# An attention and mixture-of-experts block on one core: the third batch's chain to token parts run between the second batch's expert units

## The chip, the cores and the metric

One core of a Trainium2 chip. The time is that of the whole program on the device in microseconds (us); less is better. Engines: TensorE (PE), VectorE (DVE), ScalarE (ACT), GpSimd (POOL) and SyncE (SP), which issues most of the DMAs. Each engine runs its own instructions in order and waits on semaphores for the others.

## The reference

For each of four batches of 512 tokens of width 128: causal attention with 16 heads of 8, then 16 experts of which two are mixed for each of 8 slices of 16 of a token.

```python
h = _layernorm(x) * (1 + ca) + sa
x = x + ga * _L0_attn_ref(h, Wq, bq, Wk, bk, Wv, bv, Wo, bo)     # rope, causal softmax, 16 heads
h = _layernorm(x) * (1 + cb) + sb
x = x + gb * _L0_ffn_ref(h, Wm, bm, expert_emb, W1, b1, W2, b2, Wo, bo)
# in _L0_ffn_ref:
t = (x @ Wm + bm).reshape(bs * L_ * H, HD)
w = softmax(t @ expert_emb); topw, topi = top_k(w, 2)
hmid = gelu(einsum('td,edi->tei', t, W1) + b1); eo = einsum('tei,eio->teo', hmid, W2) + b2
out = (take_along_axis(eo, topi) * topw).sum(axis=1).reshape(bs, L_, d) @ Wo + bo
```

## The kernel before

The order on each engine is written out by hand. After an opening, the kernel alternates two kinds of stage: the softmax of one batch and the expert units of the batch before it. `("loop", b)` for b = 0 and 1 is the softmax of batch b + 1 and then the expert units of batch b; `("late", 2)` is the softmax of batch 3 and then the expert units of batch 2; `("last", 3)` is the expert units of batch 3. Batches are counted from 0 in the code, so the second batch is batch 1, the third is batch 2 and the fourth is batch 3.

In a softmax stage TensorE makes scores (`big<-q_dense,k_block`) in 24 units, ScalarE takes the exponential of each into a ring of 8 buffers (L701), and TensorE weighs the values with them (`acc<-ring,vals`). Two groups of eight key blocks follow each other; `between[(g, blk)]` is a step put after the scores of block blk of group g. Between them runs what turns a batch's attention output into what its experts need, called the chain here:
- `turn_output`: TensorE transposes y (`misc<-ident,y`), VectorE copies the result to yT (L995);
- `project_out` (`misc<-wog,yT`) and `residual` (x1, L1002), `statistics` (L872 to L883), GpSimd's reciprocal root (L585), `normalise` (xn, L891 to L897);
- `turn_residual` (`misc<-ident,xn`), `modulate` (rot, L906), `tokens` (`misc<-rot,cb`; tf, L1010, cut into three bf16 parts by L910 to L913), the parts stacked by DMAs (`tstack<-tp`);
- `logits` (`misc<-cb,tf`), `route` on VectorE (L1028 to L1056, 16 instructions) with ScalarE's exponential ex (L730), `routed` (`misc<-ident,second`), wT (L1064), and 16 DMAs that spread the weights (`gm<-wT`).

In an expert stage 16 half-steps t run: TensorE makes two hidden units (`big<-tstack,w1s`), ScalarE their gelu into the ring, TensorE the outputs n = t - 2 (`acc<-ring,cb`), which VectorE (even n, L1079) or ScalarE and GpSimd (odd n, L741 and L623) multiply with the spread weights in gm. At t = 12 (`CB0_AT`) and at the end TensorE combines them (`misc<-gm,cb`), VectorE copies the result to combT (L1068), and after the last product (`misc<-wofg,combT`) VectorE adds the sum into lg (L1093) for the store. In the expert stages of batches 0 and 1 the maxima of batch b + 2 run as well, three units per half-step (`CHUNKS`): TensorE fills a bank (`misc<-k_dense,q_block`), VectorE reduces it (mx, L956). Units of all kinds share the two banks of `misc` in the order that `MISC` lists; `wait_bank_free` makes TensorE wait until the last but one use of the list is read. In the expert stage of batch 2 there are no maxima, and the chain of batch 3 (`"tail"`, `TAIL_AT`) runs there already.

The start of batch 3's softmax on VectorE (L1159 to L1171) is the yT copy, a memset of 32 rows of k_dense (L1161), the rest of the chain, the routing and the division of the attention sums. GpSimd there folds the gates: L604 and L606 (experts), L585 (the root), L592 to L595 and L612.

Of the kernel before, what the change touches and what calls it, by code (L numbers as in the profile page):

```python
# [32 lines left out]
NB, T, D = 4, 512, 128  # L33
# [6 lines left out]
NG = 2  # L40
GP = NP // NG
VW = P // GP
FH, FD, NE, FI = 8, 16, 16, 64
# [39 lines left out]
TURN_AT, ROUTE_AT = 16, 20  # L83
# [11 lines left out]
HALVES = 2 * len(STEPS)  # L95
# [15 lines left out]
TAIL_ROUTE_AT = 30  # L111
PREPARE = ["xT", "ue", "uo"]
# [23 lines left out]
at = 0  # L136
# [7 lines left out]
def opening():  # L144
# [9 lines left out]
    for k, part in enumerate(parts):  # L154
        wide = k in (1, 3)
        for use in part:
            n = len(uses)
            banks.append(n % 4 if wide else n % 2)
            if wide and banks[-1] > 1:
# [8 lines left out]
MISC = {"first": OPENING,  # L168
        "loop": ["yT", "ao"] + PREPARE + ["x1T", "tT", "lg", ("oT", 0), "wT", ("oT", 1), "v0", "v1"]
                + [use for t in range(2, HALVES + 2) for use in ["cb0"] * (t == CB0_AT) + CHUNKS[t]] + ["cb1", "fo"],  # L170
        "late": ["yT", "ao", "x1T", "tT", "lg", ("oT", 0), "wT", ("oT", 1)]
                + [("tail", use) for _, use in sorted((at, use) for use, at in TAIL_AT.items())]
                + ["cb1", ("tail", "wT"), "fo"],
        "last": ["cb0", "cb1", "fo"]}
MISC["late"] = [use if use != ("tail", "cb0") else "cb0" for use in MISC["late"]]
MISC_N = len(MISC["loop"])

MISC_START = {"first": 0, "loop": len(MISC["first"])}
MISC_START["late"] = MISC_START["loop"]
MISC_START["last"] = MISC_START["late"] + len(MISC["late"]) - MISC_N  # L180
assert MISC_N % 2 == 0

# [44 lines left out]
def build(nc, x, pack_a, pack_b, pack_c, w1_rows, shift_ones, out):  # L227
    with ExitStack() as ctx:
# [82 lines left out]
        yT_of = [yT[:, :]] * (NB - 1) + [freed[:, 0:T]]  # L311
        lg_of = [lg[:, :, :]] * (NB - 1) + [freed[:, T:2 * T].rearrange("p (n e) -> p n e", e=NE)]
# [28 lines left out]
        def use_of(here, name):  # L341
            if here[0] == "tail":
                return MISC_START["late"] + MISC["late"].index(("tail", name)) - MISC_N
            if here[0] == "second":
                return MISC["first"].index(("second", name))
            return MISC_START[here[0]] + MISC[here[0]].index(name)
# [8 lines left out]
        def wait_bank_free(eng, here, name):  # L355
# [6 lines left out]
            eng.wait_ge(s["misc_read"], here[1] * MISC_N + use_of(here, name) + 1)  # L362

        def wait_filled(eng, here, name):

            eng.wait_ge(s["misc_filled"], here[1] * MISC_N + use_of(here, name) + 1)

        def wait_read(eng, here, name):

            eng.wait_ge(s["misc_read"], here[1] * MISC_N + use_of(here, name) + 1 + CREDIT["misc_read"])  # L370
# [1243 lines left out]
```

## Time and profile before

| | |
|---|---|
| median of 3 runs | 431.77 us (429.78 to 432.44) |
| profiled execution | 431.06 us, span 429.2 us |
| mean granted TensorE clock | 0.939 |
| TensorE busy | 356.3 us (83%) |
| VectorE busy | 286.6 us (67%) |
| ScalarE busy | 257.9 us (60%) |
| GpSimd busy | 101.9 us (24%) |
| chain of waits | TensorE 54%, VectorE 15%, ScalarE 10% of the span |

How to read it: the busy shares are averages over stages with different bounds; what a step is worth is read from the timeline of its own stage. In a timeline each row is one instruction, or several alike merged (x with the count), with its start, its length, its engine, line and operands; in square brackets at the end stands how long the engine was idle before it and what ended that. A float32 matmul shows as two (x8 for four).

### The profile page before, as it was taken

To read this page: it belongs to the slowest core of one execution; us is meant where nothing else is said; L and a number is where in the kernel's file an instruction comes from. 1 tells how busy PE (TensorE), PEld (TensorE's weight loads), DVE (VectorE), ACT (ScalarE), POOL (GpSimd) and SP (SyncE) were. 2 spreads that over 40 slices of the span, in tenths; PEclk is the share of its full clock that TensorE was granted. 3 is DMA by queue.
4 is the path that set the end of the run, shared out by engine and by line. 5 is a ranking of instruction groups with operands and counts; after the bars stand their busy time and mean duration, and the time that the engine had idled before them with its cause. 6 is when DMAs were issued, how large, how long until landed. Compare 5 with 4: busy or idle time off the path is not lost.

```text
span 429.2 us, 7252 instructions
## 1 busy us (share of the span) xinstructions
PE 356.3 (83%) x2652; PEld 162.1 (38%) x2684; DVE 286.6 (67%) x593; ACT 257.9 (60%) x299; POOL 101.9 (24%) x149
## 2 busy tenths in 40 slices
PE   3745879778679889998889799998697899689994
PEld 3412434435345443433545344344354223132122
DVE  4847946888787958776676877764749247933332
ACT  9264043522247868875439858765457787858970
POOL 6080200105250204433232024431500042122000
PEclk9965868999899989999989999999989899989999
DMA  7253000003201715550105345530013256504550
GB/s 266 80 91 69 18 26 3 2 2 54 27 2 38 111 48 134 144 137 9 28 2 97 51 117 134 144 78 3 26 33 42 63 140 170 96 2 130 145 138 30
DMA packets 26991, 31.43 MB, mean 73 GB/s; under 512 B 6470, under 2 KB 17734, under 8 KB 26950
## 3 DMA queue, kind: packets, MB, share of 16 engines
q1 hardware_dynamic: 23740, 28.71, 28.7%
q0 software_dynamic: 3072, 2.13, 2.8%
q8 instruction: 21, 0.34, 0.4%
q10 hardware_dynamic: 144, 0.13, 0.1%
q14 instruction: 14, 0.11, 0.1%
HBM read 3.47 MB, written 1.05 MB: 11 GB/s over the span
## 4 chain that ended last, share of the span: by engine, by line
PE 54%; DVE 15%; ACT 10%; issue 7%; SPq 5%; DMA 5%; POOL 3%; ACTq 0%; POOLq 0%; DVEq 0%
PE acc L1193 18%; PE misc L1193 17%; PE big L1193 17%; ACT ring L701 7%; DVE mx L956 4%; PE misc L1215 2%; DVE xn L897 2%; DMA q_dense<-qk 2%; SPq L401 2%; SPq L448 2%; SPq L469 2%; DMA q_dense<-nm 1%; ACT qk_turned L709 1%; DMA gm<-wT 1%; DVE stats L872 1%
## 5 line engine op out<-in xcount | busy, mean ns | idle before, releaser
L701 ACT ACTIVATE ring<-big 128x1024 f32<-128x1024 f32 (+1 forms) x224 | 198.0, 931 | 129.5 <-PE big L1193 128.4
L956 DVE TENSOR_REDUCE mx<-misc 128x1 f32<-128x512 f32 (+7 forms) x151 | 86.1, 591 | 34.3 <-PE misc L1193 32.7
L1193 PE MATMUL acc<-ring,cb 128*32 128x512 f32 x512 | 68.8, 613 | 5.4 <-ACT ring L701 4.4
L1193 PE MATMUL big<-tstack,w1s 128*128 128x512 bf16 x177 | 54.7, 396 | 9.1 <-ACT ring L701 6.9
L1193 PE MATMUL big<-q_dense,k_block 128*128 128x448 bf16 (+7 forms) x249 | 55.0, 324 | 4.2 <-DMA gm<-qk_turned 2.0
L1079 DVE SCALAR_TENSOR_TENSOR gm<-acc,cb,gm 128x512 f32<-128x512 f32 x40 | 29.9, 747 | 27.6 <-DMA gm<-wT 20.0
L1193 PE MATMUL misc<-k_dense,q_block 128*128 128x320 bf16 (+7 forms) x168 | 42.9, 318 | 5.1 <-DVE mx L956 4.7
L1193 PE MATMUL acc<-ring,vals 128*32 128x64 f32 (+7 forms) x512 | 43.2, 436 | 0.4
L1193 PEld LDWEIGHTS big<-q_dense,k_block 128*128 128x128 bf16 x256 | 30.9, 149 | 31.0 <-ACT ring L701 14.0
L1193 PEld LDWEIGHTS misc<-k_dense,q_block 128*128 128x128 bf16 x171 | 20.7, 149 | 52.1 <-DVE mx L956 37.1
L1193 PE MATMUL big<-earlier_query,identb 128*128 128x64 bf16 (+2 forms) x176 | 37.5, 213 | 2.6 <-DMA q_dense<-nm 1.8
L623 POOL TENSOR_TENSOR gm<-osb,gm 128x512 f32<-128x512 f32 x12 | 15.6, 1298 | 93.7 <-ACT osb L741 60.7
L1193 PE MATMUL misc<-later_key,identb 128*128 128x64 bf16 (+2 forms) x151 | 32.3, 214 | 5.7 <-DMA q_block<-qk_turned 5.5
L401 POOL DMA_DIRECT2D k_block<-qk_turned x48 | 28.3, 593 | 0.5 <-issue 0.4
L1193 PEld LDWEIGHTS big<-tstack,w1s 128*128 128x128 bf16 x192 | 13.3, 98 | 33.3 <-ACT ring L701 21.8
L623 POOL TENSOR_TENSOR gm<-yT,gm 128x512 f32<-128x512 f32 x12 | 15.3, 1274 | 40.5 <-ACT yT L741 37.9
L709 ACT COPY qk_turned<-qk 128x512 bf16<-128x512 bf16 x12 | 12.2, 1088 | 14.6 <-DVE qk L913 14.6
L1193 PEld LDWEIGHTS big<-earlier_query,identb 128*128 128x128 bf16 x176 | 20.5, 116 | 1.0 <-issue 0.9
L1193 PEld LDWEIGHTS acc<-ring,cb 128*32 128x32 f32 x512 | 10.5, 108 | 26.4 <-issue 18.6
L1193 PE MATMUL misc<-tstack,gm 128*128 128x448 bf16 (+7 forms) x54 | 14.1, 316 | 6.1 <-DVE mx L956 5.8
L1193 PEld LDWEIGHTS acc<-ring,vals 128*32 128x32 f32 x512 | 11.9, 111 | 17.7 <-issue 10.9
L1193 PE MATMUL big<-k_dense,w1s 128*128 128x512 bf16 x60 | 17.5, 395 | 1.0 <-issue 0.3
(162 smaller groups left out, 457.5 us busy)
## 6 DMA issues: line engine op xcount, KB each, us to landing
gm<-wT SPq DMA_DIRECT2D x64, 256.0 KB
tstack<-tp SPq DMA_DIRECT2D x18, 128.0 KB, 4.5
q_dense<-qk SPq DMA_DIRECT2D x24, 64.0 KB
k_block<-qk_turned POOLq DMA_DIRECT2D x48, 32.0 KB, 4.3
k_dense<-qk SPq DMA_DIRECT2D x18, 64.0 KB
xs<-in_x SPq DMA_DIRECT2D x4, 256.0 KB, 8.2
ca<-in_pack_a SPq DMA_DIRECT2D x1, 769.0 KB, 7.6
q_dense<-nm SPq DMA_DIRECT2D x48, 4.0 KB, 1.8
```

Source lines behind the costliest of these rows:

```text
L401: eng.dma_start(dst[r:r + NR, :, a, :], turned).then_inc(s[f"{stack}_stacked"], 16)
L448: sp.dma_start(dst[r:r + 2 * NR, :, :], qk[j][at:at + 64, :]).then_inc(s[done], 16)
L469: sp.dma_start(q_dense[r:r + 1, GP * g:GP * g + GP, :], nm[:, g, j, BLK * a:BLK * a + BLK]).then_inc(shift_stacked[g], 16)
L623: pool.tensor_tensor(gm[:, n, :], biased[n // 2 % 2], gm[:, n, :], ALU.mult).then_inc(s["gm_ready1"], 1)
L701: act.activation(dst, src, func, scale=scale).then_inc(s["ring_read"], 1)
L709: act.copy(qk_turned[j][:, :, :], qk[j][:, :].rearrange("r (s q) -> r q s", q=BLK)).then_inc(s["qk_turned"], 1)
L872: ins = dve.bn_stats(stats[:, norm, t, :], src[:, t, :])
L897: ins = dve.tensor_scalar(xn[:, t, :], src[:, t, :], mean[:, norm, t:t + 1], rstd[:, norm, t:t + 1], ALU.subtract, ALU.mult)
L956: dve.tensor_reduce(mx[:, g, k:k + n, blk], src, AX.X, ALU.max).then_inc(s["misc_read"], 1)
L1079: dve.scalar_tensor_tensor(out=gm[:, n, :], in0=acc[:, n % 2, :], scalar=B["b2"][:, half:half + 1], in1=gm[:, n, :], op0=ALU.add, op1=ALU. ...
L1193: return pe.matmul(dst, lhsT, rhs, start=start, stop=stop)
L1215: ins = pe.transpose(bank(here, unit)[0:P, P * t:P * t + P], src, ident[:, :])
```

## The change

The chain of batch 2 from `turn_output` to `tokens` leaves batch 3's softmax. It becomes the phase `("next", 2)` and runs between the half-steps of batch 1's expert stage: on TensorE at t = 3, 6, 10 and 12 (`NEXT_AT`), on VectorE after n = 0, 3, 5, 7 and 9, GpSimd's root after its slot 5. The logits open batch 3's softmax, the weights' transposes (`routed`) come at (1, 0) of it instead of at t = 2 of batch 2's expert stage, and ScalarE's ex comes at place 8 instead of 20. yT of batch 2 lies in tf, and lg of batch 2 in the part of q_block that is free by then. SP waits for the last output of batch 1's expert stage before it stacks batch 2's parts, since both lie in tstack. The places in misc are counted through instead of by a stride of one loop turn.

```diff
-TURN_AT, ROUTE_AT = 16, 20
+TURN_AT, ROUTE_AT, ROUTE_LATE = 16, 20, 8
+NEXT_AT = {"yT": 3, "ao": 6, "x1T": 10, "tT": 12}
...
-        yT_of = [yT[:, :]] * (NB - 1) + [freed[:, 0:T]]
-        lg_of = [lg[:, :, :]] * (NB - 1) + [freed[:, T:2 * T].rearrange("p (n e) -> p n e", e=NE)]
+        yT_of = [yT[:, :]] * (NB - 2) + [tf[:, :], freed[:, 0:T]]
+        lg_of = [lg[:, :, :]] * (NB - 2) + [freed[:, T * k:T * k + T].rearrange("p (n e) -> p n e", e=NE) for k in (2, 1)]
...
             here, tail = ("late", NB - 2), ("tail", NB - 1)
+            wait_consumed(sp, experts_at(NB - 3), GROUPS["experts"] - 1)
             stack_tokens(NB - 2)
...
-                experts_out(b, K_BLOCKS)
-            here = ("late", NB - 2)
+                experts_out(b, K_BLOCKS, between={5: lambda: rsqrt(2 * NB - 2, 1)} if b == NB - 3 else {})
+            here, ahead = ("late", NB - 2), ("next", NB - 2)
             fold_experts(here)
-            rsqrt(2 * NB - 2, 1)
-            fold_out(NB - 1, here)
-            add_bias(here)
+            fold_out(NB - 1, ahead)
+            add_bias(ahead)
...
-            softmax(softmax_at(NB - 1), {ROUTE_AT: lambda: route(("late", NB - 2))})
+            softmax(softmax_at(NB - 1), {ROUTE_LATE: lambda: route(("late", NB - 2))})
...
+            def next_chain(b):
+
+                if b < NB - 3:
+                    return {}
+                after, n = ("next", b + 1), 2 * NB - 2
+                link = links("ln_link", LN_LINKS, n)
+
+                def next_residual():
+                    residual(after)
+                    statistics(x1, b + 1, n, 1, link)
+
+                return {NEXT_AT["yT"] - 3: lambda: turn_output(after), NEXT_AT["ao"] - 3: next_residual,
+                        NEXT_AT["x1T"] - 5: lambda: normalise(x1, n, 1, link),
+                        NEXT_AT["x1T"] - 3: lambda: modulate(1, hT2, after, "x1T", n),
+                        NEXT_AT["tT"] - 3: lambda: tokens(after)}
...
-                experts_out(here, experts_at(b), ahead=True)
+                experts_out(here, experts_at(b), ahead=True, between=next_chain(b))
             here = ("late", NB - 2)
-            turn_output(here)
             dve.memset(k_dense[96:P].rearrange("r h t -> r (h t)").bitcast(F32), BF16_ONES).then_inc(s["tail_ones"], 1)
-            residual(here)
-            norm_link = links("ln_link", LN_LINKS, 2 * NB - 2)
-            statistics(x1, NB - 2, 2 * NB - 2, 1, norm_link)
-            normalise(x1, 2 * NB - 2, 1, norm_link)
-            modulate(1, hT2, here, "x1T", 2 * NB - 2)
-            tokens(here)
             route(here)
+            take_weights(here)
             divide(here, NB - 1, 0)
-            take_weights(here)
...
-                experts(here, experts_at(b), NG * b + 2 * NG, ahead=True, next_sums=b + 1)
+                after = ("next", NB - 2)
+
+                def next_output():
+                    wait_read(pe, here, ("oT", 1))
+                    turn_output(after)
+
+                experts(here, experts_at(b), NG * b + 2 * NG, ahead=True, next_sums=b + 1, between={
+                    NEXT_AT["yT"]: next_output, NEXT_AT["ao"]: lambda: project_out(after),
+                    NEXT_AT["x1T"]: lambda: turn_residual(after, 2 * NB - 2),
+                    NEXT_AT["tT"]: lambda: tokens(after)} if b == NB - 3 else {})
             here = ("late", NB - 2)
-            turn_output(here)
-            softmax(NB - 1, softmax_at(NB - 1), {
-                (0, 0): lambda: project_out(here), (0, 5): lambda: turn_residual(here, 2 * NB - 2),
-                (1, 0): lambda: tokens(here), (1, 1): lambda: logits(here)})
+            softmax(NB - 1, softmax_at(NB - 1), {(0, 0): lambda: logits(here, after), (1, 0): lambda: routed(here)})
```

VectorE in batch 1's expert stage, before: the products gm of the even slots 4 and 6 with six maxima between them.

```order
L1079 SCALAR_TENSOR_TENSOR gm<-acc,cb,gm 128x512
L956 TENSOR_REDUCE mx<-misc 128x1 x4
L956 TENSOR_REDUCE mx<-misc 128x2 x2
L1079 SCALAR_TENSOR_TENSOR gm<-acc,cb,gm 128x512
L956 TENSOR_REDUCE mx<-misc 128x2 x2
```

The same place after, from the small steps that end the statistics (slot 4 follows them) to slot 6.

```order
L887 SCALAR_TENSOR_TENSOR rtmp<-rtmp 128x4
L889 SCALAR_TENSOR_TENSOR var<-var,rtmp 128x4
L1085 SCALAR_TENSOR_TENSOR gm<-acc,cb,gm 128x512
L962 TENSOR_REDUCE mx<-misc 128x1 x4
L962 TENSOR_REDUCE mx<-misc 128x2 x2
L897 TENSOR_TENSOR rtmp<-rpow 128x4
L898 SCALAR_TENSOR_TENSOR rtmp<-rtmp,var 128x4
L900 SCALAR_TENSOR_TENSOR rstd<-rtmp,rpow 128x4
L903 TENSOR_SCALAR xn<-x,mean,rstd 128x128 x4
L1085 SCALAR_TENSOR_TENSOR gm<-acc,cb,gm 128x512
```

The residual's steps stand ahead of slot 4's product, and those of normalising ahead of slot 6's, behind the same six maxima.

TensorE in batch 3's softmax at (1, 0), before: the last products of group 0, the token matmul of batch 2, then the next scores.

```order
L1193 MATMUL acc<-ring,vals 32x128 x4
L1193 MATMUL acc<-ring,vals 32x64 x4
L1193 MATMUL misc<-rot,cb 128x512
L1193 MATMUL big<-q_dense,k_block 128x448
L1193 MATMUL big<-earlier_query,identb 128x64
```

And after, the same place.

```order
L1209 MATMUL acc<-ring,vals 32x128 x4
L1209 MATMUL acc<-ring,vals 32x64 x4
L1231 MATMUL misc<-ident,second 128x128 x4
L1209 MATMUL big<-q_dense,k_block 128x448
L1209 MATMUL big<-earlier_query,identb 128x64
```

The transposes of the weights, which need the whole routing, stand where the token matmul stood.

## Rows read from the trace of the kernel before

**Rows 1.** Windows: stretch, length, busy (instructions) per engine, granted clock, DMA share, GB/s.
```profile
248.00:293.60 45.60, 43.70 (x332) 18.58 (x333) 33.94 (x64) 31.42 (x35) 16.66 (x20) 1.00 0.45 111
...
299.60:328.40 28.80, 24.12 (x234) 13.16 (x234) 20.57 (x39) 15.13 (x22) 5.56 (x8) 0.94 0.24 38
```

**Rows 2.** Timeline of TensorE, fourth batch's softmax: start, length, line, operands, idle before.
```profile
299.04 0.60 PE L1215 MATMUL misc<-ident,y 128*128 128x128 f32 x4
301.06 1.13 PE L1193 MATMUL misc<-wog,yT 128*128 128x128 f32 x8 [1.42 <-DVE yT L995]
...
311.07 0.66 PE L1215 MATMUL misc<-ident,xn 128*128 128x128 f32 x4 [2.25 <-DVE xn L897]
311.57 0.41 PE L1193 MATMUL big<-q_dense,k_block 128*128 128x128 bf16 x4
...
316.34 1.12 PE L1193 MATMUL misc<-rot,cb 128*128 128x512 f32 x2
```

**Rows 3.** Timeline (TensorE, SP) and a row of the waits, third batch's expert stage.
```profile
342.42 1.06 PE L1193 MATMUL acc<-ring,cb 128*32 128x512 f32 x8 [0.90 <-DVE gm L1079]
...
337.43 18.48 SPq L488 DMA_DIRECT2D gm<-wT  x16
...
DVE gm L1079 <- DMA gm<-wT: 5.9, 2, 3.4
```

**Rows 4.** Timeline of VectorE: residual, normalising (two places), tokens, routing.
```profile
303.23 0.69 DVE L1002 TENSOR_TENSOR x<-misc,xb 128x512 f32<-128x512 f32 x1
...
305.68 0.16 DVE L883 SCALAR_TENSOR_TENSOR var<-var,rtmp 128x4 f32<-128x4 f32 x1
...
308.07 2.95 DVE L897 TENSOR_SCALAR xn<-x,mean,rstd 128x128 f32<-128x128 f32 x4
...
317.50 0.75 DVE L1010 TENSOR_SCALAR tf<-misc,cb 128x512 f32<-128x512 f32 x1 [4.85 <-PE misc L1193]
...
320.55 0.68 DVE L1028 TENSOR_REDUCE top<-misc 128x32 f32<-128x512 f32 x1
...
331.07 1.07 DVE L1056 TENSOR_TENSOR second<-first,rtot 128x256 f32<-128x256 f32 x2
...
354.00 0.17 DVE L891 TENSOR_TENSOR rtmp<-rpow 128x4 f32<-128x4 f32 x1 [2.98 <-POOL rpow L585]
...
354.60 1.12 DVE L897 TENSOR_SCALAR xn<-x,mean,rstd 128x128 f32<-128x128 f32 x4
```

**Rows 5.** Timeline of TensorE and VectorE, second batch's expert stage.
```profile
261.10 0.60 PE L1193 MATMUL big<-tstack,w1s 128*128 128x512 bf16 x2
...
263.38 0.36 PE L1193 MATMUL misc<-k_dense,q_block 128*128 128x320 bf16 x1
...
268.73 0.46 PE L1193 MATMUL misc<-k_dense,q_block 128*128 128x128 bf16 x4
...
277.34 1.92 PE L1193 MATMUL misc<-gm,cb 128*32 128x512 f32 x16
...
280.29 0.33 PE L1193 MATMUL misc<-k_dense,q_block 128*128 128x384 bf16 x1
...
266.54 0.69 DVE L956 TENSOR_REDUCE mx<-misc 128x2 f32<-128x512 f32 x1 [0.73 <-PE misc L1193]
267.14 0.74 DVE L1079 SCALAR_TENSOR_TENSOR gm<-acc,cb,gm 128x512 f32<-128x512 f32 x1
267.80 1.01 DVE L956 TENSOR_REDUCE mx<-misc 128x2 f32<-128x384 f32 x2
```

**Rows 6.** Timeline of VectorE and GpSimd: yT copy, root, and a meeting of both.
```profile
300.27 0.68 DVE L995 COPY yT<-misc 128x512 f32<-128x512 f32 x1
...
305.92 1.03 POOL L585 TENSOR_TENSOR rpow<-var,minus_half 128x4 f32<-128x4 f32 x1 [4.34 <-DVE var L883]
...
127.21 1.01 DVE L891 TENSOR_TENSOR rtmp<-rpow 128x4 f32<-128x4 f32 x1
...
126.92 1.29 POOL L612 TENSOR_TENSOR x1b<-x,bofg 128x512 f32<-128x512 f32 x1
```

More of the change, by code:

```diff
@@ L167, with middle @@
 OPENING, OPENING_BANK, OPENING_PREVIOUS, LAST_IN_ACC = opening()
[L168 to L181, printed above, removed]
+def middle(extra):
+    uses = ["yT", "ao"] + PREPARE + ["x1T", "tT", "lg", ("oT", 0), "wT", ("oT", 1), "v0", "v1"]
+    for t in range(2, HALVES + 2):
+        uses += [("next", use) for use, at in extra.items() if at == t] + ["cb0"] * (t == CB0_AT) + CHUNKS[t]
+    return uses + ["cb1", "fo"]
+MISC = {("first", 0): OPENING, ("loop", 0): middle({}), ("loop", 1): middle(NEXT_AT),
+        ("late", NB - 2): ["lg", "wT", ("oT", 0), ("oT", 1)]
+        + [use if use == "cb0" else ("tail", use) for _, use in sorted((at, use) for use, at in TAIL_AT.items())]
+        + ["cb1", ("tail", "wT"), "fo"],
+        ("last", NB - 1): ["cb0", "cb1", "fo"]}
+MISC_START, n = {}, 0
+for phase, uses in MISC.items():
+    MISC_START[phase] = n
+    n += len(uses)
+HOSTS = {"tail": ("late", NB - 2), "next": ("loop", 1), "second": ("first", 0)}
 SOFT, EXPERT = NG * NU, len(STEPS) * EH
@@ L341, in use_of @@
         def use_of(here, name):
[L342 to L346, printed above, removed]
+            if here[0] in HOSTS:
+                host = HOSTS[here[0]]
+                return MISC_START[host] + MISC[host].index((here[0], name))
+            return MISC_START[here] + MISC[here].index(name)
         def bank(here, name):
@@ L600, in fold_experts @@
                 b = here[1]
-                pool.wait_ge(s["misc_read"], b * MISC_N + MISC_START[here[0]] + CREDIT["misc_read"])
+                pool.wait_ge(s["misc_read"], MISC_START[here] + CREDIT["misc_read"])
                 ready = s["expert_gates"]
@@ L1028, in route @@
                     link(dve.tensor_reduce(top[:, :], src, AX.X, ALU.max))
-                    if here[0] != "tail":
+                    if here[0] == "loop":
                         dve.wait_ge(s["stored"], 16 * b + CREDIT["stored"])
@@ L1357, in tokens, with logits @@
                 filled(matmul(bank(here, "tT"), B["wm"], hT2[:, :]))
-            def logits(here):
+            def logits(here, tokens_in=None):
                 wait_bank_free(pe, here, "lg")
-                wait_read(pe, here, "tT")
+                wait_read(pe, tokens_in or here, "tT")
                 for t in range(TT):
@@ L1432, in experts @@
                     elif t == 2:
-                        routed(here)
+                        if ahead:
+                            routed(here)
                         if next_sums is not None:
```

6 lines of the change are left out of this document (3 added, 3 removed).

## Prediction, made before the changed kernel was run

> **What bounds the kernel now.** I read the windows by stage first, then TensorE's timeline in the two stages that the change touches, then the timelines of VectorE and GpSimd beside it. In the second batch's expert units (248 to 293.6 us) TensorE is busy 43.70 of 45.60 us at the full clock, 2.4 GHz, and VectorE 33.94 [rows 1]. TensorE is the bound; VectorE has 11.7 us of idle time. In the fourth batch's softmax (299.6 to 328.4) TensorE is busy 24.12 of 28.80 us, and its mean granted clock is 0.94, which is some 3.5 us at the lower level, 1.2 GHz [rows 1]. Two waits in that stage are on the chain of the third batch: 1.42 us for the copy of yT and 2.25 us for xn; the low clock follows them [rows 2]. A third wait stands early in the third batch's expert units: 0.90 us for VectorE's gm, which had itself waited for the spread weights (DMA gm<-wT: 5.9 us in two waits, the longest 3.4) [rows 3]. That is what there is to win.
>
> **TensorE: what moves.** Four steps of batch 2 (counted from 0) leave the softmax for the expert units: transposes of y (0.5 us from start to next start), projection (1.0), transposes of xn (0.5), token matmul (1.0); durations 0.60, 1.13, 0.66 and 1.12 us in [rows 2]. TensorE's queue is in order and on the path in both stages, so these 3.0 us cost there what they save here. The logits stay in the softmax, now as its first step. The four transposes of the weights (about 0.5 us like those of y) move from the opening of batch 2's expert units to (1, 0) of the softmax: no difference either, -0.5 and +0.5.
>
> **Gains.** Both waits go: 1.42 + 2.25 = 3.7 us. The low clock behind them goes: 3.5 us at half rate is at most 1.7 us of work; I take 1.5, since TensorE is busy for 84% of that stage. The weights are spread during the softmax, so the 0.9 us wait goes. With the 0.5 of the transposes, 6.6 us.
>
> **Cost 1: VectorE inside the expert units.** It gets everything of the chain: yT 0.7 [rows 6], residual with statistics 2.6 (303.23 to the end of the last small one, 305.84), normalising 1.7 (354.00 to 355.72), modulating (one step over the same tile, as long as yT's), tokens with their cut into parts 3.05 (317.50 to 320.55) [rows 4]. That fits into 11.7 idle us as a sum, but not as it lies. TensorE and VectorE share two banks of misc, so TensorE can fill two units ahead of VectorE's reading and then stops. I follow the first unit that finds no bank, in the times of before:
> - Residual: the projection goes where TensorE stands at 261.10 and ends near 262.2; VectorE's block then ends at 262.25 + 2.61 = 264.9, gm takes 0.66 (start to next start), the first unit's maximum 0.5: its bank is free at 266.0. TensorE wants it at 263.38 + 1.0 = 264.4 [rows 5]. Stall 1.6 us.
> - Normalising: the last maximum before it ends at 267.23; + 1.72 + 0.66 + 0.55 = 270.15; TensorE wants the bank at 268.73 [rows 5]. Stall 1.4 us.
> - Tokens: the matmul stands at 277.34, ahead of the combination of the first halves; the block runs to 278.4 + 3.05 = 281.45, gm and the copy of combT add 1.35: 282.8. TensorE wants that bank at 280.29 + 1.0 = 281.3 [rows 5]. Stall 1.5 us.
> - yT and modulating, under 1 us each, fit: 0.3 together.
>
> Sum 4.8 us. Bounds: 2.5 if a unit's reading overlaps more than the rows say; 6.6 if the four steps of normalising take the 2.95 us that they took in the softmax, where GpSimd worked beside them, and not the 1.12 us of 354.60 [rows 4]. I take the short one: by the order GpSimd's product of slot 7 falls behind it. The reciprocal root on GpSimd now stands behind its slot 5, and var is ready near there; I see no wait.
>
> **Cost 2: a new wait at (1, 0).** TensorE's transposes of the weights now stand behind 11 us of work, and VectorE has to have the weights by then.
> - VectorE: the sum into lg ends near 300.3 (the yT copy starts at 300.27). The memset of k_dense still comes next; it ends where the residual starts, at 303.2 [rows 4], and without the copy, whose start lies 0.6 us ahead of its successor's, at 302.6 [rows 6]. Routing is 16 instructions from 320.55 to 332.14, 11.6 us [rows 4]: 314.2.
> - GpSimd now runs its seven folding steps without a pause once lg is summed, from 300.4; the window shows 5.56 us for the eight steps of the stage, of which the root of 1.0 us goes elsewhere: to about 305.0 [rows 1, 6]. A VectorE step with two inputs in SBUF waits while such a step runs: the first small step of normalising took 1.01 us and ended with GpSimd's x1b, as against 0.17 us alone [rows 4, 6]. Routing's third step meets x1b at 304.05: + 0.9 us. Weights ready at 315.1.
> - TensorE: 299.04 + 1.0 for the logits = 300.05; the work from the end of the projection, 302.0, to the wait that ended at 311.07, that is to 308.8, takes 6.8 as before: 306.85; that from 311.57 to 316.34, 4.77 at the low clock, 3.6 at the full one: 310.4 [rows 2].
>
> So it waits 4.7 us where it had waited 2.25 and 1.42. Bounds: 3.2 (no contact with GpSimd, TensorE 0.6 later) and 6.2 (the memset too waits until 305.0). A wait of 2.25 us, after 1.42, was followed by the low clock; this longer one should be too: 1.5 us, from 0.5 to 3. I see no other cover: ScalarE has nothing to do but what TensorE gives it.
>
> The page "SBUF — State Buffer" of the Trainium skill, section "Who interferes with whom", says that VectorE and GpSimd share a port pair as an exclusive lock, that a VectorE step with two SBUF inputs takes part in it against a GpSimd step that reads SBUF, and that a tensor_reduce doesn't. By that rule the first two steps of routing are free and the third one is not; the trace agrees for the small step above (1.01 us). By no lock at all the sum would be 0.9 us less.
>
> **ScalarE and the queues.** ex moves from place 20 to place 8 on ScalarE and needs lg, there at 304.1 (302.6 and the first two steps of routing, 0.7 us each). TensorE has weighting products to do between its units then, and they hide one short ScalarE step; without that cover it would cost about 1 us. On SP the six issues of token parts and 16 of weights now stand behind the wait for batch 1's last unit; behind them nothing is due before the tail. From 316 on the 16 take 18.5 us [rows 3], and the outputs, which used them behind 337 before, find nearly all landed: hidden.
>
> **Sum.** Costs 4.8 + 4.7 + 1.5 + 0.5 = 11.5; gains 6.6. Net +4.9 us on the profiled execution's 431.06 us (span 429.2): 436.0. The median of the three runs is 0.7 higher, 431.77; there it makes 436.7. I say 436.5.
>
> **Rivals.**
> 1. The idle time of VectorE takes its new work up: no stalls in the expert units. For it: 11.7 idle us against about 9 new ones. Against it: the idle lies in small pieces and the banks are two. Then -4.8: 431.9, not slower. It decides below about 1 us of stall per block. Chance 0.14.
> 2. The weights are there when TensorE comes to (1, 0), since something else (ScalarE's units) holds TensorE up in the softmax's first half. Then 4.7 and the clock's 1.5 go: 430.5. It needs TensorE 4.7 us later or VectorE's start before 299, which the logits forbid. Chance 0.10.
> 3. The third batch's expert units gain more than 0.9 us: VectorE's gm waited 5.9 us there for weights, and if that pace, and not ScalarE's and TensorE's work, set the stage, 5.9 instead of 0.9 us come back: 431.7. Against it: TensorE showed only the 0.90 us. Chance 0.09.
> 4. Worse: the long normalising and GpSimd's hold on memset and routing: 1.8 + 1.5 us more, and the low clock at 3 us: 441. Chance 0.14.
> 5. The forecast, 433.5 to 439: 0.53.
>
> Range 431 to 441. About 1% (4.3 us) is what a measurement of this kernel tells from no change; with the forecast at +4.7 it lies beside that line: slower 0.51, same 0.43, faster 0.06 (rivals 1 and 2 together, about -6).
>
> **What would show it.** In the changed profile: a TensorE wait of 3 to 6 us before misc<-ident,second in the softmax, and a granted clock below 1 after it; the waits for yT and xn gone from the softmax; second batch's expert units 51 to 55 us long instead of 45.6, with TensorE waits of about 1.5 us for VectorE's mx after the residual, xn and token parts; no wait for gm<-wT in the third batch's units. The forecast is wrong if those units stay under 50 us, if the wait at (1, 0) is under 2 us, or if the third batch's units shrink by over 3 us.

## The result, and the profile after

The changed kernel takes 436.12 us in the median of 4 runs (435.0 to 437.11); the kernel before, 430.77 us (428.97 to 432.44, 4 runs). The ratio is 1.0135, with a 95% interval from 1.0089 to 1.0181: slower, by 5.3 us. The profiled execution took 436.64 us with a span of 434.8, against 431.06 and 429.2 before, so the spans differ by 5.6 us. The forecast difference was 4.9 us.

The page of the changed kernel: span, busy time by engine, and the chain that ended last.

```profile
span 434.8 us, 7285 instructions
...
PE 360.0 (83%) x2684; PEld 161.4 (37%) x2684; DVE 284.2 (65%) x593; ACT 257.7 (59%) x299; POOL 101.9 (23%) x149
...
PE 50%; DVE 19%; ACT 11%; issue 7%; DMA 5%; SPq 5%; POOL 2%; ACTq 0%; DVEq 0%; POOLq 0%
```

No engine has more instructions than before. TensorE's busy time reads 360.0 us against 356.3, but the trace of before holds 2652 of its matmuls and this one 2684, with 2684 weight loads in both; at the mean of 0.13 us the 32 records missing there make some 4 us. What grew is VectorE's share of the chain of waits, 15% before and 19% now, while TensorE's fell from 54% to 50%. The work is the same and TensorE waits longer for VectorE.

The windows of the changed kernel: the second batch's expert units between the same instructions as the 45.60 us window of [rows 1], and the fourth batch's softmax with the opening of the third batch's units (columns as there).

```profile
248.50:302.20 53.70, 47.88 (x355) 20.41 (x352) 42.08 (x90) 31.57 (x35) 17.77 (x21) 1.00 0.37 95
...
305.80:346.00 40.20, 31.89 (x290) 16.21 (x288) 17.33 (x25) 25.80 (x35) 4.51 (x7) 0.96 0.43 98
```

The first window is 8.1 us longer than in [rows 1]. TensorE's busy time rose by 4.2 us and its idle time from 1.9 to 5.8 us. The moved work is 18 matmuls, 2.9 us from their starts to the next ones (0.47, 0.97, 0.47 and 1.03); the count rose by 23, so five records, about 1 us, are missing from the window of before, and the idle time rose by nearly 5 us rather than 3.9. VectorE got 8.1 us of work and is idle for 11.6 us, where it was idle for 11.7: none of the idle time was used up. The second stretch took 42.80 us in the kernel before, with TensorE busy for 35.60: TensorE's busy time there fell by 3.7 us and the stretch by only 2.6.

TensorE's timeline in the changed kernel: the three large waits of the expert stage, the start of the softmax, the wait at (1, 0), and the next batch's units.

```profile
267.42 0.36 PE L1209 MATMUL misc<-k_dense,q_block 128*128 128x320 bf16 x1 [1.61 <-DVE mx L962]
274.07 0.46 PE L1209 MATMUL misc<-k_dense,q_block 128*128 128x128 bf16 x4 [1.23 <-DVE mx L962]
288.79 0.38 PE L1209 MATMUL misc<-k_dense,q_block 128*128 128x384 bf16 x1 [1.44 <-DVE combT L1074]
305.73 2.03 PE L1209 MATMUL misc<-wofg,combT 128*128 128x128 f32 x16
...
323.27 1.11 PE L1231 MATMUL misc<-ident,second 128*128 128x128 f32 x4 [4.39 <-DVE second L1062]
324.18 0.58 PE L1209 MATMUL big<-q_dense,k_block 128*128 128x448 bf16 x1
...
330.80 0.44 PE L1209 MATMUL big<-q_dense,k_block 128*128 128x256 bf16 x2 [0.39 <-ACT ring L707]
...
343.06 1.07 PE L1209 MATMUL acc<-ring,cb 128*32 128x512 f32 x8
```

The waits of 1.42 and 2.25 us [rows 2] and the one of 0.90 us [rows 3] are gone. In their place stand one wait of 4.39 us and three that were not there: 1.61, 1.23 and 1.44 us.

The span by stretches, each from one instruction to the same one in both kernels (starts in TensorE's timelines):

| stretch | before | after | difference |
|---|---|---|---|
| start of the span to `misc<-ca,hT`, which opens the second batch's expert units | 247.47 | 247.91 | +0.4 |
| from there to `misc<-wofg`: the second batch's expert stage | 49.70 | 57.82 | +8.1 |
| from there to the next `misc<-ident,y`, or its place (340.00, 346.02): fourth batch's softmax and opening of the third batch's units | 42.83 | 40.29 | -2.5 |
| from there to the end of the span | 89.20 | 88.78 | -0.4 |

The sum is +5.6 us. The third stretch is worth a closer look, since its parts move in both directions:

| part of it, up to | before | after | e2_routed_late |
|---|---|---|---|
| first `128x256 bf16 x2` scores (wait 0.40 for ScalarE) | 8.95 | 6.85 | 6.85 |
| second group's first `128x448` scores | 11.18 | 11.60 | 6.25 |
| its `128x256 bf16 x2` scores | 6.16 | 6.62 | 6.32 |
| `big<-tstack,w1s` with the wait of 1.73 for ScalarE | 8.54 | 8.54 | 8.98 |
| `misc<-ident,y` | 8.00 | 6.68 | 7.90 |

The last column belongs to an experiment below.

### The profile page after: what moved, and what is told of

Same layout as the page of the kernel before. It is cut to its first block, busy times and chain, and to the rows that moved or that the text cites. A ratio compares the mean times of both kernels' runs of the same rounds, so it can differ in the third digit from the quotient of the medians.

```text
span 434.8 us, 7285 instructions
## 1 busy us (share of the span) xinstructions
PE 360.0 (83%) x2684; PEld 161.4 (37%) x2684; DVE 284.2 (65%) x593; ACT 257.7 (59%) x299; POOL 101.9 (23%) x149
## 4 chain that ended last, share of the span: by engine, by line
PE 50%; DVE 19%; ACT 11%; issue 7%; DMA 5%; SPq 5%; POOL 2%; ACTq 0%; DVEq 0%; POOLq 0%
PE acc L1209 16%; PE misc L1209 16%; PE big L1209 16%; ACT ring L707 8%; DVE mx L962 4%; PE misc L1231 2%; DMA q_dense<-qk 2%; SPq L407 2%; SPq L454 2%; SPq L475 1%; DVE xn L903 1%; DMA q_dense<-nm 1%; ACT qk_turned L715 1%; DVE gm L1085 1%; DMA gm<-wT 1%
## 5 line engine op out<-in xcount | busy, mean ns | idle before, releaser
L1209 PE MATMUL big<-tstack,w1s 128*128 128x512 bf16 x192 | 56.8, 388 | 8.1 <-ACT ring L707 7.6
L1209 PE MATMUL big<-q_dense,k_block 128*128 128x512 bf16 (+7 forms) x256 | 57.2, 327 | 6.0 <-DMA gm<-qk_turned 2.0
L1209 PE MATMUL misc<-k_dense,q_block 128*128 128x256 bf16 (+7 forms) x171 | 44.4, 322 | 14.6 <-DVE mx L962 6.5
L630 POOL TENSOR_TENSOR gm<-osb,gm 128x512 f32<-128x512 f32 x12 | 15.6, 1298 | 98.6 <-ACT osb L747 98.6
L1209 PE MATMUL misc<-tstack,gm 128*128 128x512 bf16 (+7 forms) x56 | 15.0, 320 | 6.1 <-DVE mx L962 5.8
L1209 PEld LDWEIGHTS acc<-ring,vals 128*32 128x32 f32 x512 | 11.7, 110 | 17.7 <-issue 10.9
```

What stands on the lines that cost most here:

```text
L630: pool.tensor_tensor(gm[:, n, :], biased[n // 2 % 2], gm[:, n, :], ALU.mult).then_inc(s["gm_ready1"], 1)
L1209: return pe.matmul(dst, lhsT, rhs, start=start, stop=stop)
```

## The experiments

Times are medians. The first four, the next four and the last three kernels ran as groups, each group on one chip and beside runs of the kernel before there. "The changed kernel" ran again as the first of them, so that the others have a partner. The ratios are against the kernel before.

| kernel | us | before on that chip | ratio (95%) |
|---|---|---|---|
| a0_changed | 437.07 | 429.71 | 1.0177 (1.0140 to 1.0215) |
| e2_routed_late | 431.22 | 429.71 | 1.0037 (1.0005 to 1.0069) |
| e4_thin | 436.14 | 429.71 | 1.0145 (1.0110 to 1.0181) |
| e5_thin_late | 430.65 | 429.71 | 1.0024 (0.9996 to 1.0051) |
| e1_ones_late | 435.18 | 429.48 | 1.0126 (1.0062 to 1.0190) |
| e3_even_slots | 436.89 | 429.48 | 1.0164 (1.0104 to 1.0224) |
| e6_block_n3 | 430.33 | 429.48 | 1.0006 (0.9966 to 1.0045) |
| e7_block_n4 | 431.59 | 429.48 | 1.0043 (1.0007 to 1.0080) |
| e8_pool_waits | 435.57 | 428.86 | 1.0154 (1.0107 to 1.0200) |
| e9_places | 425.81 | 428.86 | 0.9933 (0.9896 to 0.9970) |
| e10_places_all | 426.00 | 428.86 | 0.9920 (0.9887 to 0.9953) |

The theory is that of the prediction: two independent costs, a wait for the routing weights at (1, 0), and stalls because VectorE's new blocks do not fit between two banks. Its rivals were that one of the two covers the other, that the idle share of VectorE would take the blocks if they were cut or placed well, and that the loss comes from another engine.

**The changed kernel once more.**

> The changed kernel itself again, as the base for the others of this group: about 5.4 us slower than the kernel before; TensorE waits of 1.6, 1.2 and 1.4 us in the second batch's expert units and 4.4 us at (1, 0).

It had the waits of the first profile to within 0.01 us (1.61, 1.22, 1.44, 4.39), and a span of 435.2. The three waits of the expert stage came within 0.01 us in e1_ones_late, e2_routed_late and e8_pool_waits too, which have the same order there. They come from the order of the instructions and their lengths, not from chance.

**The wait at (1, 0): taken away.** The transposes of the weights go four places later, past the rest of the second group's scores.

```diff
-            softmax(NB - 1, softmax_at(NB - 1), {(0, 0): lambda: logits(here, after), (1, 0): lambda: routed(here)})
+            softmax(NB - 1, softmax_at(NB - 1), {(0, 0): lambda: logits(here, after), (1, 4): lambda: routed(here)})
```

> The weights' transposes come at (1, 4) of the fourth batch's softmax instead of (1, 0); nothing else. Theory (the wait at (1, 0) is lost whole, and the low clock comes from it): the wait of 4.4 us goes and the clock stays at 1.0 in that stage, 5.5 us less than the changed kernel, so level with the kernel before within 1 us. Rival (the softmax is paced by ScalarE or the wait moves to a later place): under 2 us less than the changed kernel.

TensorE's timeline in this kernel has the transposes without a wait:

```profile
303.54 2.03 PE L1209 MATMUL misc<-wofg,combT 128*128 128x128 f32 x16
...
324.99 0.66 PE L1231 MATMUL misc<-ident,second 128*128 128x128 f32 x4
...
339.84 0.66 PE L1231 MATMUL misc<-ident,y 128*128 128x128 f32 x4
```

The stretch from the first to the last of these rows is 36.30 us, 3.99 less than in the changed kernel, and the expert stage kept its 57.83 us. By the table of parts, 5.65 us went where the wait and the low clock behind it had been (11.60 to 6.25 and 6.62 to 6.32), 0.44 came back with the transposes' new place, and 1.22 came back in the opening, where this execution had the low clock and that of the changed kernel had not. The medians, which average over that, differ by 5.85 us in this group; by the ratios of the changed kernel's two measurements (1.0135 and 1.0177) it is 4.2 to 6.0. 6.2 were priced for the wait and the clock, 5.5 expected. So one number in the order carries most of the loss; 1.5 us against the kernel before are left.

**The two halves of the routing's lateness.** In one kernel the memset stands behind the copy of the weights. In the other, GpSimd's folding steps are held back until the routing is over.

```diff
-            dve.memset(k_dense[96:P].rearrange("r h t -> r (h t)").bitcast(F32), BF16_ONES).then_inc(s["tail_ones"], 1)
             route(here)
             take_weights(here)
+            dve.memset(k_dense[96:P].rearrange("r h t -> r (h t)").bitcast(F32), BF16_ONES).then_inc(s["tail_ones"], 1)
```

> The memset of k_dense stands behind the copy of wT instead of ahead of routing; nothing else of the changed kernel differs. Theory (VectorE's queue up to the weights sets the wait at (1, 0)): routing starts 2.2 us earlier, but all of GpSimd's folding now runs beside it, which may take up to 1 us back; the wait falls from 4.4 to 2.2 to 3.2 us, and 1.2 to 2.2 us are gained. Rival (something else ends the wait): no difference.

TensorE's row there:

```profile
321.78 0.66 PE L1231 MATMUL misc<-ident,second 128*128 128x128 f32 x4 [3.01 <-DVE second L1062]
```

4.39 became 3.01 us, inside what was expected. The median is 1.9 us below that of a0_changed from the other group, and the two intervals overlap, so a gain in time is not resolved.

```diff
+            pool.wait_ge(s["w_ready"], NB - 1)
             fold_out(NB - 1, ahead)
             add_bias(ahead)
```

> The changed kernel, with GpSimd's last four folding steps held until the weights of batch 2 are ready. Theory (the third step of routing took 1.50 instead of 0.69 us since GpSimd's x1b ran beside it): that step takes 0.69 us, the wait at (1, 0) falls from 4.39 to 3.6 us, 0.8 us in all. Rival (the step is long for another reason): it stays at 1.50 us and the wait at 4.39.

VectorE's third step of the routing, in the changed kernel, then in this one, and TensorE's wait in this one:

```profile
311.56 0.69 DVE L1037 TENSOR_TENSOR q_block<-misc,top 128x512 f32<-128x512 f32 x1
312.28 1.50 DVE L1039 SCALAR_TENSOR_TENSOR first<-q_block,cb 128x512 f32<-128x512 f32 x1
```

```profile
309.39 0.69 DVE L1040 SCALAR_TENSOR_TENSOR first<-q_block,cb 128x512 f32<-128x512 f32 x1
```

```profile
319.58 1.09 PE L1232 MATMUL misc<-ident,second 128*128 128x128 f32 x4 [3.59 <-DVE second L1063]
```

In the changed kernel GpSimd's product for x1b starts at 311.95 and takes 1.28 us, to 313.23; VectorE's step is the only one of the routing that it meets with two inputs in SBUF, and that step ends at 313.78. With GpSimd quiet it takes 0.69 us, and TensorE's wait falls by 0.80. The page "SBUF — State Buffer" of the Trainium skill, section "Who interferes with whom", says that a step of VectorE with two SBUF inputs and a GpSimd step that reads SBUF take turns at one lock, and that a tensor_reduce takes no part. Here the runs agree: 0.81 us for one meeting, and the tensor_reduce of 310.83, beside GpSimd's product for xb (310.70 to 311.99), kept its 0.69 us. The median, 1.5% above before, doesn't resolve a gain in time.

**The stalls in the expert stage.** Three kernels change how VectorE's blocks lie there. The first moves three of the four steps one half-step, so that the blocks follow the other bank.

```diff
-NEXT_AT = {"yT": 3, "ao": 6, "x1T": 10, "tT": 12}
+NEXT_AT = {"yT": 3, "ao": 7, "x1T": 11, "tT": 13}
```

> The places of the chain are 3, 7, 11 and 13 instead of 3, 6, 10 and 12, so every block of VectorE stands behind an even slot and ahead of an odd one, where VectorE has no product gm of 0.66 us to do; the blocks are as long as before. Theory (a bank is late by the block and what is queued behind it): each of the three waits is shorter by 0.5 to 0.7 us, some 1.8 us in all. Rival (only the block's own length counts): no difference.

TensorE's timeline there, the three waits:

```profile
269.50 0.44 PE L1209 MATMUL misc<-k_dense,q_block 128*128 128x256 bf16 x2 [0.83 <-DVE mx L962]
...
276.44 0.44 PE L1209 MATMUL misc<-k_dense,q_block 128*128 128x512 bf16 x1 [1.21 <-DVE mx L962]
...
292.11 0.36 PE L1209 MATMUL misc<-k_dense,q_block 128*128 128x320 bf16 x1 [1.43 <-DVE mx L962]
```

The wait after the residual halved, as the theory said; the other two stayed as they were, which it did not say. The stage from the first transposes to `misc<-wofg` fell from 51.71 to 50.84 us, not by the 1.8 expected, and the median shows no gain. The timelines show what stood against the other two gains. The first small step of normalising now starts at 273.45 beside GpSimd's product of 273.22 and takes 1.06 us, where it took 0.15 in the changed kernel. And the token matmul now stands behind the combination of the first halves: TensorE wants its bank 2.4 us after that matmul instead of 3.1, while VectorE, with gm and the copy of combT no longer behind the block, frees it only 0.8 us sooner after the block's start.

The second cuts the blocks into twelve pieces, one in each gap between units, each planned at 1.2 us at most. The cut in the code:

```diff
-                        NEXT_AT["tT"] - 3: lambda: tokens(after)}
+                        ...
+                    split(dve.tensor_tensor(rest[:, :], tf[:, :], tp[0][:, :], ALU.subtract))
+                    yield
+                    split(dve.tensor_copy(tp[1][:, :], rest[:, :]))
+                    dve.tensor_tensor(tp[2][:, :], rest[:, :], tp[1][:, :], ALU.subtract).then_inc(s["tp_ready"], 1)
+                    yield
+
+                step = steps()
+                return {at: lambda: next(step) for at in (0, 2, 3, 4, 5, 6, 7, 8, 9, 10, 11, 12)}
```

> The chain stays between the second batch's expert units, but VectorE's blocks are cut into twelve pieces of at most 1.2 us behind slots 0 and 2 to 12 (projection at half-step 5, transposes of xn at 12, token matmul at 13). Theory (the cost there is the length of a block against two banks): the waits of 1.6 + 1.2 + 1.4 us shrink to under 1.5 us in all, about 3 us less than the changed kernel. Rival (it is the sum of VectorE's work that counts, or TensorE's own 3 us): the stage keeps its 53.7 us, no gain.

The large stalls are gone (1.61, 1.23 and 1.44 became waits of 0.15 to 0.38 us, with one exception), but the median is only 0.9 us below that of a0_changed and the stage only 1.2 us shorter, where 3 was expected. The exception, in the timelines of this kernel: GpSimd's folding step, VectorE's rows beside it, and TensorE.

```profile
291.12 1.27 POOL L630 TENSOR_TENSOR gm<-osb,gm 128x512 f32<-128x512 f32 x1 [3.68 <-ACT osb L747]
```

```profile
276.29 1.32 DVE L1187 TENSOR_SCALAR xn<-x,mean,rstd 128x128 f32<-128x128 f32 x2
...
291.16 1.52 DVE L1203 CAST tp<-rest 128x512 bf16<-128x512 f32 x1
```

```profile
294.06 0.39 PE L1257 MATMUL misc<-k_dense,q_block 128*128 128x192 bf16 x2 [1.28 <-DVE mx L962]
```

The cast of one part of the tokens takes 0.43 us elsewhere in this execution (286.21) and 1.52 us here, where GpSimd's product starts 0.04 us ahead of it. The pair of xn at 276.29 takes 1.32 instead of 0.59 us, with GpSimd's product of 276.00 beside it. Two small steps met GpSimd's products as well: the one at 264.70 took 1.00 instead of 0.17 us, the one at 270.54 took 0.75 instead of 0.15. So cutting the blocks into pieces spread them over more of GpSimd's steps, and the four meetings took some 3.2 us of VectorE's time, where the blocks of the changed kernel meet none. The cast accounts for the stall of 1.28 us; how much of the rest between the 1.2 and the 3 us expected is due to the other three was not traced.

The third has the pieces, the transposes at (1, 3), and the memset behind the copy of the weights.

```diff
-(1, 0): lambda: routed(here)
+(1, 3): lambda: routed(here)
```

> The twelve pieces, the weights' transposes at (1, 3), and the memset of k_dense behind the copy of wT. Theory (both costs are separate and both lie on the path): 8.5 us less than the changed kernel, 3 us less than the kernel before. Rival (one covers the other): no more than the better of the two alone, so no faster than the kernel before.

It takes 430.65 us, 6.4 below a0_changed where 8.5 were expected, and 0.9 above the kernel before where 3 less were expected; the interval of the ratio holds 1. Against e2_routed_late it is 0.6 us less, and the two intervals overlap, so the medians don't tell "both costs add" from "no more than the better of the two". The timelines do: the expert stage from `misc<-ident,y` to the unit behind the last large wait takes 42.40 us, as in e4_thin, and the stretch of softmax and opening 35.59 us, where e2_routed_late has 36.30 and the changed kernel 40.29. Each saving stands in its own stage. The whole expert stage is even so 59.15 us long in this execution, since the granted clock was 0.50 from 298 to 304 us; in e4_thin, at the full clock, it is 56.61.

**A block by itself, in the kernel before.** To measure a stall without the chain, twelve statistics instructions whose results nobody uses are put behind VectorE's slot 3 or 4 of the second batch's units (`between={3: block_alone}` or `{4: block_alone}`).

```diff
+                def block_alone():
+                    for i in range(3):
+                        for t in range(TT):
+                            dve.bn_stats(ex[:, TT * i + t, 0:6], x1[:, t, :])
```

> The kernel before with 12 needless statistics steps on VectorE (2.6 us, their results are not used) behind slot 3 of the second batch's expert units. Theory (two banks): last read 261.8 + 2.6 + 0.66 for gm + 0.5 = 265.5 against TensorE's want at 263.4: 2.1 us slower. Rival (the 11.7 us of VectorE's idle time in that stage take it up): no difference.

> The kernel before with the same 12 needless statistics steps one slot later, behind slot 4 and ahead of the odd slot 5. Theory (two banks, and what is queued behind the block): 264.4 + 2.6 + 0.5 = 267.5 against 266.0: 1.5 us slower, 0.6 less than behind slot 3. Rival (idle time takes it up): no difference; (only the length counts): as behind slot 3.

VectorE's block behind slot 3 and TensorE's next wait; then TensorE's wait in the kernel with the block behind slot 4:

```profile
261.57 2.41 DVE L1161 BATCH_NORM_STATS2 ex<-x 128x6 f32<-128x128 f32 x12
...
265.08 0.36 PE L1198 MATMUL misc<-k_dense,q_block 128*128 128x320 bf16 x1 [1.84 <-DVE mx L956]
```

```profile
267.51 0.44 PE L1198 MATMUL misc<-k_dense,q_block 128*128 128x256 bf16 x2 [1.00 <-DVE mx L956]
```

A block of 2.4 us costs a wait of 1.84 us behind slot 3 (2.1 expected) and 1.00 us behind slot 4 (1.5 expected), in a stage where VectorE is idle for a quarter of the time. The stage from `misc<-ca,hT` to `misc<-wofg` grew by 1.92 us in the first (49.70 to 51.62) and by 1.08 us in the second (to 50.78). So the mechanism holds without the chain, and with idle time on VectorE in the same stage. The whole kernel tells less. The first ratio, 1.0006, is 0.3 us, and its interval ends at 1.9, below the 2.1 expected; the second, 1.0043, is 1.8 us from an interval of 0.3 to 3.4. In both profiles the yT wait of the softmax had shrunk from 1.42 to 1.06 us, which takes 0.36 us of the stall back; the 1.6 us that are then left of the first lie inside its interval.

**Another way to the same gain.** The waits that the change removes are waits of TensorE for VectorE inside the softmax. In the kernel before, the steps of the chain can go a few places later there, with no work moved between stages.

```diff
-                (0, 0): lambda: project_out(here), (0, 5): lambda: turn_residual(here, 2 * NB - 2),
-                (1, 0): lambda: tokens(here), (1, 1): lambda: logits(here)})
+                (0, 2): lambda: project_out(here), (1, 0): lambda: turn_residual(here, 2 * NB - 2),
+                (1, 1): lambda: tokens(here), (1, 2): lambda: logits(here)})
```

> The kernel before, not the changed one, with TensorE's four steps of batch 2's chain at later places of the same softmax: projection at (0, 2), transposes of xn at (1, 0), token matmul at (1, 1), logits at (1, 2). Theory (the two waits were TensorE's own order, and VectorE has the time for the chain there): the waits of 1.42 and 2.25 us go, and where the clock fell after them it stays up: 3.5 to 5 us less than the kernel before, without one VectorE step in the expert units. Rival (the chain itself is the bound; whatever TensorE does meanwhile, it waits for xn or later for the weights): the waits come back at (1, 0) or ahead of the third batch's first outputs, under 1.5 us gained.

TensorE's timeline in it:

```profile
300.87 1.16 PE L1193 MATMUL misc<-wog,yT 128*128 128x128 f32 x8
...
310.01 0.66 PE L1215 MATMUL misc<-ident,xn 128*128 128x128 f32 x4 [0.51 <-DVE xn L897]
...
336.69 1.06 PE L1193 MATMUL acc<-ring,cb 128*32 128x512 f32 x8 [0.88 <-DVE gm L1079]
```

The yT wait is gone, that for xn fell from 2.25 to 0.51 us (xn takes 2.96 us here, as in [rows 4], beside GpSimd), and the wait for gm, 0.88, stays. The kernel takes 425.81 us against 428.86 in the same group: 0.9933, from 0.9896 to 0.9970. That is 3.05 us, under the 3.5 to 5 expected, with an interval of 1.3 to 4.5. In its profile the stretch of softmax and opening is 38.43 us against 42.83, 4.4 us less: the two waits make 3.2, and the granted clock stays at 1.00 from 308 to 314, where the low clock had cost the kernel before 1.3 us. It is faster than the kernel before and than the changed one, and with the next kernel the best of all that were run.

The same for the softmaxes inside the loops:

```diff
-                    (0, 0): lambda: project_out(here), (0, 3): lambda: norm1(here, 2 * b + 2),
-                    (0, 4): lambda: project(here), (0, 6): lambda: turn_residual(here, 2 * b + 3),
+                    ("scores", 0, 5): lambda: project_out(here), ("scores", 0, 8): lambda: norm1(here, 2 * b + 2),
+                    (0, 5): lambda: project(here), (0, 6): lambda: turn_residual(here, 2 * b + 3),
```

> As the kernel with later places, and the same in the softmax stages of the second and third batch: projection behind the sixth score unit, first transposes of xn behind the ninth, projection of queries and keys one block later. Theory: the waits of 0.83 and 1.61 us (second batch) and 1.06 and 1.84 us (third) shrink, 1 to 4 us less than with the last stage alone. Rival (there VectorE's chain to the stacked queries and token parts ends last, and it starts later now): no further gain, or a loss of about 1 us per stage.

It takes 426.0 us, the same as e9_places: the 1 to 4 us expected did not come. Yet the waits did shrink. That for yT went from 0.83 to nothing and from 1.06 to 0.19 us, that for xn from 1.62 to 1.30 and from 1.85 to 1.56. Of these 1.15 and 1.16 us only a part arrives: from `misc<-ident,y` to the token matmul the second batch's softmax takes 17.56 us instead of 18.08, and the third batch's 17.78 instead of 18.51. In this execution 0.8 us was lost again at the opening of the first batch's expert units, where the granted clock fell to 0.74 (155 to 160 us), which it did not in that of e9_places. A gain of 1.2 us is not resolved by the medians.

## Why the prediction was right

The forecast was 436.5 us, range 431 to 441, and the measured median is 436.12. Slower was the likelier direction, with the ratio just over the line of 1%. By stages the forecast of +4.9 us is 7.8 for the expert stage, -2.0 for softmax and opening and -0.9 behind them; the profiles have 8.1, -2.5 and -0.4, and 0.4 us ahead of the change, which it does not touch. Point by point:

**Gains, 6.6 us forecast.** The waits of 1.42, 2.25 and 0.90 us went as forecast. VectorE's gm in the third batch's units now starts without a wait for a transfer:

```profile
344.19 0.75 DVE L1085 SCALAR_TENSOR_TENSOR gm<-acc,cb,gm 128x512 f32<-128x512 f32 x1 [0.21 <-PE acc L1209]
```

The low clock that followed the xn wait cost 1.3 us in that execution, against the 1.5 forecast: from `misc<-ident,xn` to 323.46 us it took 12.39, and 12.55 in e7_block_n4, but 11.13 in e6_block_n3, where the same wait of 2.25 us was not followed by it. So this gain was there in two executions of three. The opening lost 0.43 us with the transposes of the weights, as forecast (7.11 us in e6_block_n3 and 6.68 in the changed kernel, both at the full clock).

**The moved work, and the logits: the step that failed.** The prediction lets the token matmul's 1.0 us come back whole, and says that the logits stay in the softmax, now as its first step, without a price for the new place. The two stood at (1, 0) and (1, 1), and taking both away from there shortened the softmax by less than one of them. TensorE's rows of the second group's scores, in the kernel before, and in e2_routed_late, where the logits are gone from there and the clock is full:

```profile
317.52 0.39 PE L1193 MATMUL big<-q_dense,k_block 128*128 128x448 bf16 x1
...
318.40 1.13 PE L1193 MATMUL misc<-cb,tf 128*128 128x128 f32 x8
...
320.34 1.82 PE L1193 MATMUL acc<-ring,vals 128*32 128x512 f32 x16
```

```profile
317.56 0.41 PE L1209 MATMUL big<-q_dense,k_block 128*128 128x448 bf16 x1 [0.22 <-ACT ring L707]
...
319.26 0.38 PE L1209 MATMUL big<-q_dense,k_block 128*128 128x384 bf16 x1 [0.26 <-ACT ring L707]
...
319.84 1.82 PE L1209 MATMUL acc<-ring,vals 128*32 128x512 f32 x16
```

ScalarE's units set the pace there: it works through seven of them without a pause (315.04 to 320.75) in the second kernel, and TensorE waits for it. Without the 1.0 us of logits that part is 6.32 us long instead of 6.16. Over both parts, from the wait of 0.40 for ScalarE to the next one, e6_block_n3 takes 16.09 us at the full clock. Less the wait for xn (2.25) and its transposes (0.5) that is 13.34, against 12.57 in e2_routed_late: 1.9 us of TensorE's work are gone and 0.8 is gained. The table's part of the second group's scores tells the same: 6.32 us with neither step, 6.16 with the logits, and 7.19 in e9_places with the logits and the token matmul. ScalarE's pace covers one of the two steps and not both. As the softmax's first step the logits cost their 0.9 us. So the softmax shrank by some 1.1 us less than the sum says.

**Cost 1, 4.8 us forecast.** The stalls were forecast at 1.6, 1.4, 1.5 and 0.3 us and came as 1.61, 1.23, 1.44 and 0.22: 4.5 us. The stage grew by 8.1 us, where moved work and stalls made 7.8. The third of them ends with the copy of combT, as the sum has it, and not with a maximum, as the list of signs says. The choice of the short normalising was right: its four steps, in VectorE's timeline, after the residual's product and maxima.

```profile
266.13 0.16 DVE L889 SCALAR_TENSOR_TENSOR var<-var,rtmp 128x4 f32<-128x4 f32 x1
266.22 0.75 DVE L1085 SCALAR_TENSOR_TENSOR gm<-acc,cb,gm 128x512 f32<-128x512 f32 x1
266.89 2.04 DVE L962 TENSOR_REDUCE mx<-misc 128x1 f32<-128x320 f32 x4
...
271.77 1.12 DVE L903 TENSOR_SCALAR xn<-x,mean,rstd 128x128 f32<-128x128 f32 x4
```

TensorE's unit of 267.42 starts 0.53 us after the maxima's row begins, that is when the first of its four has been read. This is the step of the sum "its bank is free", and the row answers it.

**Cost 2, 4.7 us forecast.** The wait is 4.39 us. Of its parts: the memset starts at 309.04 after 0.48 us in which VectorE waits for nothing that the profile shows, and ends at 310.80; the routing takes 310.83 to 323.21, with 0.81 us for the meeting with GpSimd where 0.9 was forecast. Counted from the end of the product with wofg (307.60, in the sum 299.04), the weights are ready after 15.6 us, forecast 16.1, and TensorE comes for them after 11.3, forecast 11.4.

```profile
309.04 1.76 DVE L1183 MEMSET k_dense<- 32x2048 f32 x1 [0.48 <-issue]
310.83 0.69 DVE L1034 TENSOR_REDUCE top<-misc 128x32 f32<-128x512 f32 x1
```

**The low clock behind it, 1.5 us forecast.** It came: windows of the changed kernel, with the granted clock before the last two figures.

```profile
320.00:324.00 4.00, 0.73 (x4) 0.73 (x5) 3.08 (x6) 0.00 (x0) 0.00 (x0) 0.87 0.00 0
324.00:328.00 4.00, 3.64 (x22) 1.69 (x24) 0.69 (x1) 2.69 (x4) 0.00 (x0) 0.70 0.21 65
...
336.00:340.00 4.00, 2.22 (x18) 0.96 (x16) 0.78 (x2) 3.97 (x6) 0.00 (x0) 1.00 0.53 146
```

The transposes and the scores at 1.2 GHz take 7.53 us (323.27 to 330.80); at the full clock 0.5 and 6.32 make 6.8. It costs 0.7 us, not 1.5: the same ScalarE pace hides a part. The term was too high by 0.8, inside its bounds of 0.5 to 3. In the opening, after a wait of 1.73 us for ScalarE that both kernels have, the low clock came in the profile of before (0.60 from 332 to 336) and not in that of after (1.00 from 336 to 340). It is worth 0.9 to 1.3 us there, and that is chance: with the same wait it came in e1 to e5 and e8 to e10 and stayed out in a0, e6 and e7.

Together, the stretch of softmax and opening should have shrunk by 2.0 us by the sum and shrank by 2.5. The 1.1 us overlooked with the logits and 0.2 of the first low clock's gain count against it; the opening's 0.9, the smaller wait (0.3) and the cheaper clock (0.8) count for it: 2.7 in all. The total came out right within 1 us partly because these offset each other, and that part is luck.

**ScalarE and the queues, nothing forecast.** ex comes at 313.01, 0.63 us, and TensorE's wait for ScalarE stays 0.39 us, before 0.40. The 16 issues of the weights now take SP from 325.14 on, for 18.68 us, and no wait for them shows.

**The rivals.** The first (VectorE's idle time takes the blocks) fell with the windows: the idle time is the same as before to 0.1 us. The second (weights there in time) fell with the wait of 4.39. The third (the third batch's units gain the 5.9 us that VectorE's gm waited) fell too: from the `acc<-ring,cb` at 337.04 (343.06) to the `misc<-ident,xn` of the tail at 355.77 (361.07) the units gained 0.7 us. The fourth, the long normalising, didn't come.

## What to carry to other kernels

Idle share is no room: when two engines share two buffers, cost each block put on the reader by the first unit that finds no free buffer (a block of 2.4 us stalled the writer for 1.0 to 1.8 us beside a quarter of idle time). A step that needs the end of a long chain belongs where that chain ends. A step that lies where another engine sets the pace can be free there and cost its whole length elsewhere (here one step of 1.0 us, not two). Before moving work between stages, try the consumer a few places later inside its stage: four changed places gave 0.7% here with no work moved.

## What the runs showed of the hardware that was not expected

- Cutting VectorE's blocks made them meet GpSimd more often: a cast took 1.52 instead of 0.43 us and a pair of tensor_scalars 1.32 instead of 0.59 us when GpSimd's product had started just ahead of them. The forecast had a meeting for one step only, 0.9 us, measured 0.81.
- The low clock (1.2 GHz) came after the waits of 3.0 to 4.4 us in all six executions, after 2.25 us in two of three, and after 1.7 us in the opening in nine of thirteen. It cost 0.5 to 0.8 us after the wait at (1, 0), 0.9 to 1.3 in the opening and 1.3 to 1.4 after the wait for xn; after the wait at (1, 0) ScalarE's pace hid a part. In e5_thin_late it came at the end of the expert stage, after waits of 1.27 and 0.16 us that left the clock at 1.00 in e4_thin, and cost 2.5 us. Between kernels with the same instructions ahead, `misc<-ca,hT` of the second batch's units started up to 3.2 us apart (245.02 to 248.18 us), so the spans of two single executions do not resolve 1 to 2 us; the lengths of one stage at one clock do.
- A memset of 32x2048 f32 took 1.76 us and began 0.48 us after VectorE was free.
